# Half-slot side work in an attention phase, the square root beside the other table, and an overlapped start of the second phase

## The reference

```python
x = L0_attn_z
x = x + _layernorm(_L0_attn_ref(_layernorm(x), ln_scale, ln_bias, w_qkv, w_proj, b_proj))  # 16 heads of 8, softmax over 512 keys, z + out
x = x + _layernorm(_L0_ffn_ref(_layernorm(x), kernel, s_in, s_k, bias))                    # bf16, fp8 grid, one 128x128 product
x = x + _layernorm(_L1_attn_ref(_layernorm(x), ...))   # hawk block:
#   xn = rmsnorm(x); gate, xc = split(xn @ W_in.T)     xc = conv4(xc)
#   alpha = exp(-8 softplus(fb) sigmoid(xc @ Wf)); beta = sqrt(1 - alpha**2 + 1e-6)
#   h = scan(alpha, beta * sigmoid(xc @ Wi) * xc);     x = x + (gelu(gate) * h) @ W_out.T
#   then rmsnorm, gelu(mgate) * mx, W_shrink, added
x = x + _layernorm(_L1_ffn_ref(_layernorm(x), ...))    # 8 experts by argmax, capacity 100 each, one shared weight
```

## Time and profile before

| what | us |
|---|---|
| median of 3 runs (1431.35 to 1436.4) | 1431.36 |
| the profiled execution | 1437.65 |
| its span, first to last instruction | 1435.9 |
| first to last exponential of attention | 71.7 to 914.3 |
| PE, DVE, ACT, POOL busy | 1220.5, 1160.6, 968.2, 824.6 |

### The profile page before, as it was taken

One profiled execution on the slowest core, in us unless ns is written; L12 is line 12 of the kernel. 1 busy time (PEld: TensorE's weight loads), 2 busy tenths in 40 slices (PEclk: granted clock), 3 DMA queues, 4 the chain that ended last, 5 costly groups with the idle time before them and its releaser, 6 DMA issues.

```text
span 1435.9 us, 26041 instructions
## 1 busy us (share of the span) xinstructions
PE 1220.5 (85%) x8624; PEld 492.4 (34%) x8624; DVE 1160.6 (81%) x2518; ACT 968.2 (67%) x1653; POOL 824.6 (57%) x1068
## 2 busy tenths in 40 slices
PE   1499899899899999999999999856999899899853
PEld 0123233233233233233233223323545545545533
DVE  2668889889889889889989988433789889889874
ACT  1177777777777777877877878555767667666630
POOL 5303554654654654655555444634677877877763
PEclk7589999999999999999999989888999999999975
DMA  1121101101101101101100100000000000000000
GB/s 56 50 83 42 35 31 42 36 31 41 37 31 42 37 31 40 38 30 41 39 30 32 34 14 3 1 0 1 1 8 16 8 8 16 8 8 16 8 8 22
DMA packets 52517, 37.87 MB, mean 26 GB/s; under 512 B 8864, under 2 KB 51744, under 8 KB 52384
## 3 DMA queue, kind: packets, MB, share of 16 engines
q1 hardware_dynamic: 52384, 36.22, 7.9%
HBM read 6.31 MB, written 4.19 MB: 7 GB/s over the span
## 4 chain that ended last, share of the span: by engine, by line
PE 33%; DVE 23%; POOL 20%; issue 13%; SPq 5%; ACT 5%; POOLq 0%; DMA 0%; ACTq 0%; DVEq 0%
DVE neg_max L473 11%; PE bank L201 10%; PE bank L182 9%; SPq L621 4%; PE bank_pair L169 4%; ACT probs L348 3%; PE bank L210 3%; POOL probs L1154 2%; PE bank L272 2%; POOL x_all L1148 2%; POOL zn L1146 1%; POOL rs_t L1088 1%; POOL probs L1119 1%; POOL rs_x L1088 1%; POOL rs_h L1116 1%
## 5 line engine op out<-in xcount | busy, mean ns | idle before, releaser
L473 DVE TENSOR_REDUCE neg_max<-bank_pair 128x2 f32<-128x1024 f32 x512 | 615.5, 1215 | 120.7 <-PE bank_pair L169 115.9
L348 ACT ACTIVATE probs<-bank 128x512 f32<-128x512 f32 x1024 | 558.5, 596 | 113.2 <-PE bank L182 108.6
L182 PE MATMUL bank<-q_stack,k_stack 50*128 50x512 bf16 x1024 | 362.3, 390 | 36.4 <-ACT probs L348 19.3
L201 PE MATMUL bank<-probs,v_pad 128*32 128x256 f32 x4096 | 331.4, 396 | 2.7 <-ACT outT L306 2.3
L169 PE MATMUL bank_pair<-k_stack,q_stack 48*128 48x512 bf16 x1024 | 293.8, 397 | 31.0 <-DMA k_stack<-k_parts 15.7
L182 PEld LDWEIGHTS bank<-q_stack,k_stack 50*128 50x128 bf16 x1024 | 83.6, 93 | 301.2 <-ACT probs L348 228.6
L201 PEld LDWEIGHTS bank<-probs,v_pad 128*32 128x32 f32 x4096 | 81.1, 108 | 175.6 <-issue 156.0
L724 PE MATMUL bank_pair<-probs,w_gates 128*128 128x512 f32 x256 | 122.7, 624 | 16.7 <-DVE probs L1046 8.9
L522 POOL TENSOR_TENSOR f_b<-f_bf,ffn_bias 128x512 bf16<-128x512 bf16 x16 | 18.9, 1182 | 157.3 <-ACT f_bf L353 157.3
L169 PEld LDWEIGHTS bank_pair<-k_stack,q_stack 48*128 48x128 bf16 x1024 | 54.0, 94 | 60.5 <-DVE neg_max L473 41.2
L1154 POOL TENSOR_TENSOR probs<-probs 128x1024 f32<-128x1024 f32 x16 | 37.7, 2354 | 62.9 <-DVE probs L1068 62.9
(11 more groups left out here) (232 smaller groups left out, 2252.6 us busy)
## 6 DMA issues: line engine op xcount, KB each, us to landing
q_stack<-q_parts SPq DMA_DIRECT2D x384, 32.0 KB
k_stack<-k_parts SPq DMA_DIRECT2D x384, 32.0 KB
x_all<-in_z_dram SPq DMA_DIRECT2D x16, 256.0 KB, 2.8
out_dram<-x_all SPq DMA_DIRECT2D x16, 256.0 KB, 2.3
q_stack<-max_rows SPq DMA_DIRECT2D x64, 8.0 KB
w_gates<-in_w_gates_dram SPq DMA_DIRECT2D x1, 512.0 KB, 3.7
w_in<-in_w_in_dram SPq DMA_DIRECT2D x1, 256.0 KB, 2.7
w_grow<-in_w_grow_dram SPq DMA_DIRECT2D x1, 256.0 KB, 3.8
```

Of the source, the lines that this page charges most:

```text
L182: nc.tensor.matmul(st_ps[h][:, :], k_stack[par][rows, p, c * P:(c + 1) * P], q_stack[par][rows, p, :], start=True, stop=True).then_inc(s[" ...
L201: mm = nc.tensor.matmul(acc[32 * g:32 * g + 32, cols], v_pad[bpar][:, kc, 4 * a + g, :], probs[:, at + g, cols], start=(t == 0 and kc == 0 ...
L348: nc.scalar.activation(probs[:, 4 * (n % RING) + g, :], st_ps[g % 2][:, :], ACT.Exp, scale=SCALE)\
L473: nc.vector.tensor_reduce(neg_max[j // 4][:, c, j % 4, :], score_ps[c % 2][:, :, :], AX_X, ALU.max, negate=True).then_inc(s["max_read"], 1)
```

## The change

The half slot becomes the unit: `u = 2 * slot + half`, 0 to 31. Four things change.

1. In attention, the side work is laid out by `u` on PE, ACT and DVE. Products that were one block of 1.1 us are cut in two halves that stand behind two units (proj 8 and 9, v 17 and 18, q 21 and 22, k 25 and 26). `MISC` has a new cyclic order, and POOL's blocks stand in another order. SP's copies of a half stack are cut into q and k, and the maxima's two copies stand between them.
2. The last attention iteration (15) is taken out of `iterate` and gets `extra` work between its units: the second phase's iterations -1 and 0 for batch 0 up to the gelu of the gate (`early_*`), its statistics for batch 1, `in_tap` and the soft constants. Between tails 16 and 17 only iteration 1 is left.
3. In the second phase the root comes ahead of the first gelu, so that the two gelus stand together, and the preload goes.
4. The transposes of the norm for batch 0 use `pair1` instead of `bank_t`.

```diff
-    MISC = [("yT", -2, s["yT_ready"], 1, 1), ("ffn", -2, s["ffn_read"], 1, 1), ("o1", -1, s["o_nat_ready"], 2, 2),
-            ("v", 1, s["v_ready"], 2, 2), ("oT", -1, s["oT_ready"], 1, 1), ("proj", -1, s["att_ready"], 1, 1),
...
+    MISC = [("o1", -1, s["o_nat_ready"], 2, 2), ("oT", -1, s["oT_ready"], 1, 1), ("proj", -1, s["att_ready"], 1, 1),
+            ("maxT1", 0, s["maxT_read"], 2, 2), ("yT", -2, s["yT_ready"], 1, 1), ("ffn", -2, s["ffn_read"], 1, 1),
...
+        def features(n, half):
+            cols = slice(half * (T // 2), (half + 1) * (T // 2))
+            mm = nc.tensor.matmul(bank_of(n, i)[:, cols], w[n][:, :], znT[:, cols], start=True, stop=True)
+            if half == 1:
+                mm.then_inc(s[n + "_ps"], 1)
...
+            if u in (8, 9) and live(i, -1):
+                if u == 8:
+                    wait(pe, s["oT_ready"], i - 1 + 1)
+                    wait_misc_free(pe, i, "proj")
+                tokens("proj", oT, w["proj"], (0, 1) if u == 8 else (2, 3), s["proj_ps"])
...
         for slot in range(2 * NP):
...
+            for half in range(2):
+                u = 2 * slot + half
+                score_t(slot, 2 * half)
+                score_max(slot // 2, 2 * (slot % 2) + half)
+                score_t(slot, 2 * half + 1)
+                if u == 13 and live(i, 0):
+                    max_t(1, i)
+                if u == 29 and live(i, 1):
+                    max_t(0, i + 1)
+                prob_v(slot, half)
+                side_product(u)
+                if extra:
+                    extra(u)
...
+                (behind if g % 2 else between)(u)
+                if extra and g % 2:
+                    extra(u)
...
         load_x(sp, i + 3)
         if live(i, 1):
-            stack_half(1, i + 1, 1 - par)
+            stack_half("q", 1, i + 1, 1 - par)
         if live(i, 0):
             max_rows_out(1, 0)
+        if live(i, 1):
+            stack_half("k", 1, i + 1, 1 - par)
         if live(i, 2):
-            stack_half(0, i + 2, par)
+            stack_half("q", 0, i + 2, par)
         if live(i, 1):
             max_rows_out(0, 1)
+        if live(i, 2):
+            stack_half("k", 0, i + 2, par)
...
-            nc.scalar.preload_act_table_set("gelu_and_others")
...
+        if live(i, -1):
+            b = i - 1
+            wait(act, s["om_ready"], b + 1)
+            A(beta, beta, ACT.Sqrt, bias=consts["tiny"][:, 0:1]).then_inc(s["beta_ready"], 1)
         if live(i, -2):
             b = i - 2
             wait(act, s["mg_ps"], b + 1)
             wait(act, s["shrink_ps"], b)
             A(grown, pair1[:, :, :], ACT.Gelu).then_inc(s["mg_ready"], 1)
-        if live(i, -1):
-            b = i - 1
-            wait(act, s["om_ready"], b + 1)
-            A(beta, beta, ACT.Sqrt, bias=consts["tiny"][:, 0:1]).then_inc(s["beta_ready"], 1)
...
+    def early_tensor(pe, u):
+
+        if u == 14:
+            wait(pe, s["xn_ready"], 1)
+            wait(pe, sems["max_read"], 32 * NB)
+            for c in range(C):
+                mm = nc.tensor.transpose(pair1[:, 0, c * P:(c + 1) * P], xn[:, c * P:(c + 1) * P], consts["ident"][:, :])
+            mm.then_inc(s["xT_ps"], 1)
+        if u == 17:
+            wait(pe, s["xT_ready"], 1)
+            wait(pe, s["taps_set"], 1)
+        if 17 <= u < 17 + TAPS:
+            tap = u - 17
+            nc.tensor.matmul(pair0[:, 0, :], w["in_tap"][:, tap, :], xT_pad[:, tap:tap + T],
+                             start=(tap == 0), stop=(tap == TAPS - 1))
+        if u == 17 + TAPS:
+            nc.tensor.matmul(pair0[:, 1, :], w["in"][:, 0, 3 * P:4 * P], xT, start=True, stop=True)\
+                .then_inc(s["xc_ps"], 1)
+        if u in (27, 28):
+            n = u - 27
+            if n == 0:
+                wait(pe, s["conv_init"], 2)
+            mm = nc.tensor.matmul(pair0[:, n, :], w["in"][:, 0, n * P:(n + 1) * P], xT, start=True, stop=True)
+            if n == 1:
+                mm.then_inc(s["gate_ps"], 1)
...
+            att["last"](pe, att["tensor"], early)
             att["tail"](pe, att["tensor"], NB)
             layer1["all_free"](pe)
-            pe.wait_ge(loaded1, LOADED1)
-            pe.wait_ge(soft_step, SOFT + 4)
-            pe.wait_ge(pool_set1, POOL_SET1 + 2)
-            layer1["begin"](pe, layer1["tensor"], range(-1, 2))
+            pe.wait_ge(soft_step, SOFT + 3)
+            layer1["begin"](pe, layer1["tensor"], range(1, 2))
```

More of the change, by code:

```diff
@@ L257, in side_product @@
                 transpose4(lambda c: zn[:, c, :], consts["ident"][:, :], misc, P, s["znT_ps"])
-            if slot == 5 and live(i, -1):
-                wait(pe, s["oT_ready"], i - 1 + 1)
-                wait_misc_free(pe, i, "proj")
-                for c in range(C):
-                    mm = nc.tensor.matmul(misc[:, c * D:(c + 1) * D], oT[:, c * P:(c + 1) * P], w["proj"][:, :],
-                                          start=True, stop=True)
-                mm.then_inc(s["proj_ps"], 1)
@@ L266, in side_product @@
-            if slot in (7, 9) and live(i, 2):
-                n = "q" if slot == 7 else "k"
-                wait(pe, s["znT_ready"], i + 2 + 1)
-                if bank_of(n, i) is misc:
-                    wait_misc_free(pe, i, n)
-                nc.tensor.matmul(bank_of(n, i)[:, :], w[n][:, :], znT[:, :], start=True, stop=True).then_inc(s[n + "_ps"], 1)
-            if slot == 10 and live(i, 0):
+            for n, first in (("q", 21), ("k", 25)):
+                if u in (first, first + 1) and live(i, 2):
+                    if u == first:
+                        wait(pe, s["znT_ready"], i + 2 + 1)
+                        if bank_of(n, i) is misc:
+                            wait_misc_free(pe, i, n)
+                    features(n, u - first)
@@ L319, in side_read, with read_hi @@
-            if slot == 4 and live(i, -1):
+            src = misc[:, :].rearrange("p (cu t g d) -> p cu t g d", t=2, g=4, d=HD)
+            dst = v_pad[1 - par][:, :, :, :].rearrange("p c (u t g) e -> p (c u) t g e", u=2, t=2)
+            nc.scalar.activation(dst[:, :, t, :, 16 * t:16 * t + HD], src[:, :, t], ACT.Copy).then_inc(s["v_ready"], 1)
+        def read_hi(n, parts):
+            wait(act, s[n + "_ps"], i + 2 + 1)
+            for half in range(2):
+                wait(act, s[f"{n}{half}_ready"], 16 * STACK_DMAS * (i + 2))
+            nc.scalar.activation(parts[:, 0, :], bank_of(n, i)[:, :], ACT.Copy).then_inc(s[n + "_hi"], 1)
@@ L320, in side_read, with read_all, between @@
+        def read_all(n, rest):
+            wait(act, s[n + "_lo"], 3 * (i + 2))
+            nc.scalar.activation(rest[:, :], bank_of(n, i)[:, :], ACT.Copy).then_inc(s[n + "_hi"], 1)
+        def between(u):
+            if u == 7 and live(i, -1):
                 wait(act, s["oT_ps"], i - 1 + 1)
@@ L434, in between, with behind @@
+        def behind(u):
+            q = s["quant_step"]
+            b = i - 2
+            if u == 0 and live(i, -2):
                 wait(dve, q, 9 * b + 5)
@@ L436, in between @@
                     .then_inc(q, 1)
-            if slot == 2 and live(i, -2):
-                b = i - 2
+            if u == 2 and live(i, -2):
                 wait(dve, q, 9 * b + 6)
@@ L441, in between @@
                     .then_inc(q, 2)
[L442 to L443 removed]
+            if u == 8 and live(i, -2):
                 wait(dve, q, 9 * b + 8)
@@ L474, in vector @@
                                             negate=True).then_inc(s["max_read"], 1)
-                (side if c % 2 else between)(2 * p + c // 2)
+                behind(C * p + c)
+                if extra:
+                    extra(C * p + c)
     def first_stats(dve):
@@ L1283, in _ @@
             att["iterate"](sp, att["sync"], 0)
+            att["last"](sp, att["sync"])
             for i in (NB, NB + 1):
```

538 lines of the change are left out of this document (288 added, 250 removed).

## The result

| what (medians, us) | before | after |
|---|---|---|
| timed runs | 1431.49 | 1413.44 (1412.17 to 1416.51) |
| the profiled execution, its span | 1437.65, 1435.9 | 1412.17, 1410.3 |
| first product of slot 0, of slot 8 in iteration 0 | 71.09, 98.64 | 62.58, 89.59 |
| gate's gelu of batches 1, 4, 15 | 969.10, 1055.59, 1349.57 | 937.10, 1025.00, 1324.66 |

The ratio is 0.9868 (0.9845 to 0.9892): 1.3% faster, 18 us. The forecast was 41, to 1390, and its range ended at 1413. So the direction came true and the size did not: less than half of it came.

A forecast was written before the change was run, and what follows sets the result against it. No engine alone was taken as the bound; in attention, side work overran the two-deep buffers' slack. Terms -5 - 32.4 - 4.7 + 6.2 - 6.7 + 1.5 = -41.1 gave 1396.5 profiled, 1390 median; 80% range 1374 to 1413.

The forecast's parts named there:

- start, to iteration 1: Start of attention: slot 0 no longer waits behind k's copies, part given back to heavier side work in iteration 0; -5 us.
- twelve steady iterations: Steady attention: the period falls from 53.5 to 50.8 us, 12 x -2.7 = -32.4 us.
- iterations 13 and 14: Late attention: some side work is gone in both orders, so less is to be won; -4.7 us.
- iteration 15: Last attention iteration: added products and reads are hardly hidden, as PE is over 90% busy; +6.2 us, bounds 4 and 9.
- turn, to batch 1's gate: From the last exponential to batch 1's gate gelu: batch 0's work no longer stands there; -6.7 us, bounds 0 to -13.
- second phase, to batch 15's gate: Second phase: the removed load gives nothing, the root's new place costs +0.13 an iteration; +1.5 us in all.
- `mx` (now 1212.90) moves about 2.5 later ... which absorb it: Second phase: the root delays `mx` by 2.5 us; waits of 1.41 and 0.85 behind it absorb all but 0.13 an iteration.
- B: Rival, second phase: late `mx` holds `forget` and `w_out`, costing 8.5 us instead of 1.5, about 1397; chance 10%.
- Halves of 0.58 fit in slack which a block of 1.16 overran: Steady attention on PE: cutting side products in halves gives part of the 2.7 us won per iteration.
- the walk: Unit-by-unit walk of attention's new order: excess of 11.6 us over 39.2, giving a steady period of 50.8, 0.8 either way.
- The median is 6.3 below the profiled execution before; taken the same: Final step: the profiled execution of 1396.5 us is turned into a median of 1390 by the same distance.
- rival A: Steady attention: spreading gives little, the period stays at 53.3, some 30 of the 41 us are lost, about 1420; chance 13%.

The follow-up runs named there:

- root_only: The kernel before with only the second phase's new ACT order, the root ahead of the first gelu: 1441.77 us, ratio 1.0076.

## Why the prediction was wrong

The terms of the sum, each measured between the same marks in the changed kernel and in each of the two traces of before. The forecast rests on the first; iteration 15 and the turn are parted at the accumulator's read.

| term | forecast | against the first trace | against the second |
|---|---|---|---|
| start, to iteration 1 | -5 | -5.5 | -2.6 |
| twelve steady iterations | -32.4 | -25.6 | -25.6 |
| iterations 13 and 14 | -4.7 | -1.1 | +1.6 |
| iteration 15 | +6.2 | +7.1 | +7.1 |
| turn, to batch 1's gate | -6.7 | -6.9 | -9.1 |
| second phase, to batch 15's gate | +1.5 | +7.1 | +7.7 |
| end | 0 | -0.7 | +2.3 |
| sum | -41.1 | -25.6 | -18.6 |

On its own trace the forecast misses 15.5 by three terms, and the rest of the 23 by the step from there to the median.

*The second phase (5.6; 6.2 by the second trace).* The step "`mx` (now 1212.90) moves about 2.5 later ... which absorb it" had the waits right: 2.38 was measured, and with PE kept busy the phase was the old one but for 1 us. What failed is that a pause was priced as a pause. Before, PE's idle time stood in pieces of 1.43 and less; where it stood in one piece of 2.38, the clock fell three times in eleven iterations, and `mx` took up to 1.6 longer (3.56 against 1.98). It is a mechanism that I did not have among the rivals; of those, B named the right place, and nearly the right price (8.5), with the wrong cause.

*The steady iterations (6.8).* The mechanism was right and the size was off. "Halves of 0.58 fit in slack which a block of 1.16 overran": a half takes 0.65 to the next product, not 0.58, and the whole one 1.09. Eight halves explain 0.43 of the 0.57 that the period is above the walk. The rest isn't traced to a place. The forecast also gave the halves a part of the gain; they had none. Two thirds of the gain were the one wait. (The slots listed in the forecast add up to 11.7 to 11.9 and not to 11.6, which is 0.1 to 0.3 of the same gap.)

*Iterations 13 and 14 (3.6; 6.3 by the second trace).* "Less is to be won" was a guess where a walk was needed. With q's and k's products gone, DVE's quantization, split and division, all now behind units 24 to 31, set the pace: iteration 14 takes 50.3 at full clock, when the old order needs 48.5, or 47.1 with `att` early.

*From the profiled execution to the median (7.6).* "The median is 6.3 below the profiled execution before; taken the same": it came out 1.3 above it. Before's traced execution lay above its median and after's lay below. The distance of one execution from its median didn't carry over to the next kernel. Measured from one traced execution to the other the change is worth 25.5, not 18.

*What the second trace changes.* The start was right to 0.2 us for slot 0 (62.58 against 62.4) and 0.4 for slot 8 (89.59 against 90.0). By iteration 1 the traces of kernels with before's SP order stand at 123.9 to 126.8, so a term of -2.6 or of -5.5 depends on which of them is taken. It is the same behind batch 15's gate: 83.3 and 86.3 in the two traces of before, 85.6 in the changed kernel. At the end no gain or loss is shown.

What held: no wait for `att` or `max_parts`, the maxima's rows in time, and iteration 15 and the turn in size. These two need a word. By the forecast's own mark, the last exponential, iteration 15 is 6.1 longer (forecast 6.2) and the turn 5.9 shorter (forecast 6.7). The forecast's 6.7 isn't what its steps give: 35.7 to 30 is 5.7, and an accumulator's read that comes 1.0 later takes nothing off that stretch. Nor was its step right:

```profile
920.43 1.04 POOL L1123 TENSOR_TENSOR probs<-probs,rs_x 128x512 f32<-128x512 f32 x1
```

`xn` of batch 1 was ready 33.2 behind the last exponential and not 30, and the stretch from there to the gate's gelu took 15.6 instead of 19.0, which the forecast didn't have. That the turn's size came out is in part luck. So is rival A's time (1420 for 1413), which came from another cause.

## What to carry to other kernels

Find the one instruction that a shared buffer waits for before respreading everything: one instruction's place was worth 19 us, the rest of the new order 8 in the twelve steady iterations. Don't cut products that PE has to run anyway when PE is as busy as here (48.5 of 50.9 us). When a wait of PE is moved, ask whether pauses merge: idle time that costs nothing in pieces may cost 1.6 us in one, by the clock behind it. Walk the first and last iterations of a pipeline as well as a middle one. And take two traces of the kernel before, where a few microseconds matter.

## What the hardware showed that was not expected

- In the changed kernel's eleven iterations `mx` waited 2.38 in eight and 1.63 in three. The granted clock fell to 0.50 at three of the eight pauses of 2.38 and at the last one of 1.62 (at 1324.34, where `mx` took 3.51), and at none once two idle products had cut the pause to 1.08.
- A shorter pause can be followed by a fall as well. The wait of 1.43 for `att` was followed within 1 to 2 us by 10 us at half clock in iteration 14 of the first trace of before, by 3.4 us in iteration 13 of the second, and by 3.3 us once in the steady stretch of root_only (358.7 to 362.0); in the steady iterations of before's two traces nothing followed it.
- The two traces of before differ at the start, in iterations 13 and 14, in the turn and at the end, where the clock falls at other places in each, and not in the steady stretches. Over 17 runs it ranged from 1427.48 to 1435.89. That the falls make all of this is argued, not shown.
- `y_q` on DVE took 0.68 in the second trace of before (at 441.58) and takes 1.40 to 1.75 in the new place (the 1.75 at 832.51 beside an operation of POOL from 832.44 to 833.71), while `y_grid` fell from 0.97 to 0.62 in a steady iteration. The forecast put the sum of such changes at 0; these two make +0.4 on DVE.
